# Attention's PSUM banks given out one by one, with the two sub-heads as separate steps in a new order

## The reference, cut to what matters

```python
attn1 = _attn(q1, k1, v)            # softmax(q1 k1^T / 4) v
attn2 = _attn(q2, k2, v)
attn = attn1 - lambda_full * attn2
rms = jax.lax.rsqrt(jnp.mean(attn * attn, axis=-1, keepdims=True) + EPS)
attn = attn * rms * subln_w * (1.0 - LAMBDA_INIT)
return attn.reshape(b, t, 512) @ wo.T
```

## Time and profile before

| what | value |
|---|---|
| median of three runs | 2588.03 us (2586.67 to 2591.05) |
| the profiled execution: own time, span | 2588.56 us, 2586.8 us |
| mean granted TensorE clock | 0.974 |
| busy share of the span: PE, DVE, ACT, POOL | 94%, 66%, 46%, 7% |
| heads of L0's attention (first exponential to last) | 184 to 1071 us |
| heads of L1's attention | 1847 to 2432 us |
| page, exponentials (line 565) | 896, 932 ns each on average |
| page, sums (line 494) | 2 x 3584 records, 560 ns each |

### The profile page before, as it was taken

The page is one execution under the profiler, slowest core; times in us unless marked ns, Lnnn a source line. Parts: engine busy times, 40 slices in busy tenths (PEclk is TensorE's granted clock), DMA queues, the critical chain, the costliest instruction groups (busy, mean ns, idle before and its releaser), DMA issues. The chain is left out here.

```text
span 2586.8 us, 41795 instructions
## 1 busy us (share of the span) xinstructions
PE 2424.4 (94%) x15600; PEld 1274.4 (49%) x15600; DVE 1705.7 (66%) x3976; ACT 1178.8 (46%) x1571; POOL 186.2 (7%) x341
## 2 busy tenths in 40 slices
PE   6899999999999999888999999968899999999886
PEld 5662333333333333367888888757533333333465
DVE  2247888888888888483444444442478888888586
ACT  2125656556656656652222122231255555555553
POOL 3000000000000000100000000000011111111103
PEclk9899999999999999899999999979899999999998
DMA  5654222122222200001000000005512122210001
GB/s 192 152 127 94 44 26 26 26 40 36 26 26 26 26 2 2 30 1 49 25 25 24 24 24 24 1 0 150 107 37 36 24 39 39 39 21 2 26 1 66
DMA packets 56669, 108.96 MB, mean 42 GB/s; under 512 B 11820, under 2 KB 22060, under 8 KB 56488
## 3 DMA queue, kind: packets, MB, share of 16 engines
q1 hardware_dynamic: 53960, 96.84, 19.0%
q0 software_dynamic: 2528, 9.70, 1.1%
HBM read 73.75 MB, written 31.46 MB: 41 GB/s over the span
## 5 line engine op out<-in xcount | busy, mean ns | idle before, releaser
L565 ACT ACTIVATE l_w_hi_prob<-l_p_work 128x1024 f32<-128x1024 f32 (+2 forms) x896 | 802.1, 932 | 535.4 <-PE l_p_work L472 535.3
L617 DVE TENSOR_REDUCE l_maxima<-l_p_ring 128x1 f32<-128x512 f32 x1280 | 824.3, 686 | 201.4 <-PE l_p_ring L447 179.5
L494 PE MATMUL l_p_work<-l_w_hi_prob,v_all 128*32 128x512 f32 (+3 forms) x3584 | 860.1, 560 | 8.7 <-ACT l_w_hi_sums L556 1.5
L494 PE MATMUL l_p_work<-l_w_hi_prob,l_ones 128*32 128x512 f32 (+3 forms) x3584 | 854.7, 560 | 0.0
L447 PE MATMUL l_p_ring<-xT_all 48*128 48x512 f32 (+3 forms) x1680 | 375.4, 443 | 11.9 <-DVE l_maxima L614 11.9
L447 PEld LDWEIGHTS l_p_ring<-xT_all 48*128 48x128 f32 x1680 | 157.6, 184 | 427.7 <-DVE l_maxima L617 244.0
L472 PE MATMUL l_p_work<-xT_all 50*128 50x512 f32 (+3 forms) x1680 | 325.3, 407 | 0.2 <-DMA xT_all<-l_shift_rows 0.2
L614 DVE CUSTOM_DVE_ANT_0 l_masked_scores<-l_p_ring,l_mask 128x128 bf16<-128x128 f32 (+3 forms) x512 | 230.7, 488 | 88.3 <-PE l_p_ring L447 79.0
L494 PEld LDWEIGHTS l_p_work<-l_w_hi_prob,v_all 128*32 128x32 f32 x3584 | 148.1, 108 | 282.6 <-issue 180.2
L472 PEld LDWEIGHTS l_p_work<-xT_all 50*128 50x128 f32 x1680 | 157.8, 185 | 186.7 <-ACT l_w_hi_prob L565 103.5
L1085 DVE SCALAR_TENSOR_TENSOR ffn_h<-ffn_p_u,ffn_group_scales,ffn_silu 128x512 f32<-128x512 f32 x64 | 48.1, 751 | 213.7 <-PE ffn_p_u L214 207.9
(11 more groups left out here) (149 smaller groups left out, 2870.9 us busy)
## 6 DMA issues: line engine op xcount, KB each, us to landing
xT_all<-q_parts SPq DMA_DIRECT2D x180, 128.0 KB
q_parts<-l_part SPq DMA_DIRECT2D x64, 256.0 KB
xT_all<-k_parts SPq DMA_DIRECT2D x90, 128.0 KB
k_parts<-l_part SPq DMA_DIRECT2D x40, 256.0 KB
xT_all<-k_parts SPq DMA_DIRECT2D x90, 64.0 KB
x<-in_x_T SPq DMA_DIRECT2D x4, 1024.0 KB, 11.2
x<-in_L_attn_x POOLq DMA_DIRECT2D x1, 4096.0 KB, 16.2
out<-x SPq DMA_DIRECT2D x16, 256.0 KB, 2.0
```

The lines of the kernel that those rows point to most:

```text
L494: summing = pe.matmul(p_out[r0:r0 + VD, off:CH], lhs, prob[step % PRING][:, sub, off:CH], start=first, stop=final)
L565: act.activation(prob[step % PRING][:, :, off:CH], p_score[:, step % 2, :, off:CH], ACT.Exp, scale=HD ** -0.5).then_inc(exped, 1)
L617: dve.tensor_reduce(to, scores, AX.X, ALU.max).then_inc(freed, 1)
```

## The change

- Every item that took two banks is now two items of one bank. `pair` becomes `maxima` of one sub-head (letters Q for sub-head 0, R for sub-head 1, P still for both); `score` takes a sub-head (letters U and V take the next one, S two). Each of these matmuls now waits and signals by itself.
- Banks: `p_ring` has four instead of three; scores have three single banks instead of two times two; `p_out` one. In the projections, q, k and value tiles share one ring of four work banks instead of three and two.
- The exponential is one instruction of up to 128 x 512 for each sub-head, twice as many as before. `prob` still has four buffers of both sub-heads, and a sum waits for both.
- `sums` has a buffer for each query half, so `copy_out` waits for the transposes of the same half one head earlier; the copies stand 4 and 3 half-steps (L0) or 3 and 2 (L1) behind.
- `keep` does one multiplication over both sub-heads (256 elements) instead of two (128 each).
- New order strings. Played out, one steady head of L0 has 16 sums in 10 runs of W (before: 16 runs), 64 row-half matmuls in 11 runs of R (before: 32 groups in 16 runs), and the two turns next to each other. One head of L1 has 12 sums in 8 runs of W (before: 9) and its row halves in 9 runs of R (before: 11).

```diff
-RING = 3
+RING = 4
+SCORE_BANKS = 3
+WORK_BANKS = 4
-QK_BANKS = 3
-V_BANKS = 2
...
+        done = {"score": [SUM_LAG] * 2, "maxima": [self.first_pairs] * 2, "sum": 0, "shift": 1}
...
+                if what in "SUV":
+                    for _ in range(2 if what == "S" else 1):
+                        take("score", S, 0 if done["score"][0] == done["score"][1] else 1)
+                elif what in "PQR":
+                    for sub in {"P": (0, 1), "Q": (0,), "R": (1,)}[what]:
+                        take("maxima", U, sub)
...
+L0 = Layer("l0", D, D, False, "VUQWWPRSUWRQVQVVWRQRUUQWUUURRQWQURSQWWXURUVRQWUVRQVQWWRVRQSWWQVSPTTRVSWWWVQR",
+           24, (4, 3))
+L1 = Layer("l1", D // 4, D // 4, True, "PVRWSQVTQRVUVRWWWUUQRVQWRURWXQRUQUVWRUQVWUVURQRQWTQVRVUWWWQUV",
+           20, (3, 2))
...
+            def take_bank(item):
+
+                if L.bank_at[item] >= RING:
+                    pe.wait_ge(freed, L.bank_at[item] - RING + 1)
+
+            def pair(n, u, subs=(0, 1)):
...
+                for sub in subs:
+                    take_bank(("maxima", n, u, max(subs)))
...
                 filling.then_inc(filled, 1)
...
-                if step >= 2:
-                    pe.wait_ge(exped, step - 1)
-                for sub in range(2):
-                    rows = slice(HALF * sub, HALF * sub + FROWS)
-                    scoring = pe.matmul(p_score[:, step % 2, sub, off:CH],
-                                        k[i][rows, L.k_head(n), kt * P:(kt + 1) * P],
-                                        q[i][rows, n % 2, qc * CH + off:(qc + 1) * CH], start=True, stop=True)
-                scoring.then_inc(scored, 1)
+                i, at = slot(n // 2), 2 * (n * S + s) + sub
+                if at < SCORE_BANKS:
+
+                    pe.wait_ge(v_kept, NT - WORK_BANKS + 1 + at)
+                else:
+                    pe.wait_ge(exped, at - SCORE_BANKS + 1)
+                if s == 0 and sub == 0:
+                    pe.wait_ge(shift_in, 64 * (n + 1))
+                rows = slice(HALF * sub, HALF * sub + FROWS)
+                pe.matmul(p_score[:, at % SCORE_BANKS, off:CH], k[i][rows, L.k_head(n), kt * P:(kt + 1) * P],
+                          q[i][rows, n % 2, qc * CH + off:(qc + 1) * CH], start=True, stop=True).then_inc(scored, 1)
...
-                if n + qc:
-                    before = ("turn", n, qc - 1) if qc else ("turn", n - 1, QC - 1)
-                    act.wait_ge(filled, L.filled_at[before])
-                act.activation(sums[:, :], p_out[:, :], ACT.Copy).then_inc(out_copied, 1)
+                if n:
+                    act.wait_ge(filled, L.filled_at["turn", n - 1, qc])
+                act.activation(sums[:, qc, :], p_out[:, :], ACT.Copy).then_inc(out_copied, 1)
...
-                act.activation(prob[step % PRING][:, :, off:CH], p_score[:, step % 2, :, off:CH], ACT.Exp,
+                act.activation(prob[step % PRING][:, sub, off:CH], p_score[:, at % SCORE_BANKS, off:CH], ACT.Exp,
                                scale=HD ** -0.5).then_inc(exped, 1)
...
-                dve.tensor_tensor(half[:, 0, :, :], cols[:, :, 0, 0:VD], recip[:, :, 0:1].to_broadcast([P, QPC, VD]),
-                                  ALU.mult)
-                dve.tensor_tensor(half[:, 1, :, :], cols[:, :, 1, 0:VD], recip[:, :, 1:2].to_broadcast([P, QPC, VD]),
+                dve.tensor_tensor(half[:, :, :, :], cols[:, :, :, 0:VD], recip[:, :, :, :].to_broadcast([P, QPC, 2, VD]),
                                   ALU.mult).then_inc(freed, 1)
```

More of the change, by code:

```diff
@@ L104, in __init__ @@
         self.filled_at, self.bank_at = {}, {}
-        bank = 0
+        bank = fills = 0
         for item in self.items:
-            if item[0] in ("pair", "shift", "turn"):
-                self.bank_at[item] = bank
-                self.filled_at[item] = len(self.bank_at)
-                bank += 2 if item[0] == "pair" else 1
+            if item[0] == "pair":
+                self.bank_at["maxima", *item[1:], 0], self.bank_at["maxima", *item[1:], 1] = bank, bank + 1
+                fills += 1
+                self.filled_at["maxima", *item[1:], 0] = self.filled_at["maxima", *item[1:], 1] = fills
+                bank += 2
+            elif item[0] in ("maxima", "shift", "turn"):
+                fills += 1
+                self.bank_at[item], self.filled_at[item] = bank, fills
+                bank += 1
     def projections(self):
@@ L139, in heads, with take @@
         S, U = len(self.steps), len(self.pairs)
-        out, scores, sums, pairs, shifts = [], 0, 0, self.first_pairs, 1
-        turns = []
-        while scores < SUM_LAG:
-            out.append(("score", *divmod(scores, S)))
-            scores += 1
+        done = {"score": [SUM_LAG] * 2, "maxima": [self.first_pairs] * 2, "sum": 0, "shift": 1}
+        out, turns = [("score", *divmod(i, S), sub) for i in range(SUM_LAG) for sub in range(2)], []
+        def take(name, size, sub):
+            at = done[name][sub]
+            done[name][sub] += 1
+            if at < HEADS * size:
+                out.append((name, *divmod(at, size), sub))
         for _ in range(HEADS):
             for what in self.pattern:
-                if what == "S" and scores < HEADS * S:
-                    out.append(("score", *divmod(scores, S)))
-                    scores += 1
-                elif what == "P" and pairs < HEADS * U:
-                    out.append(("pair", *divmod(pairs, U)))
-                    pairs += 1
-                elif what == "X" and shifts < HEADS:
-                    out.append(("shift", shifts))
-                    shifts += 1
+                if what in "SUV":
[4 more added lines that the diff above has]
+                        take("maxima", U, sub)
+                elif what == "X" and done["shift"] < HEADS:
+                    out.append(("shift", done["shift"]))
+                    done["shift"] += 1
                 elif what == "T" and turns:
@@ L538, in _ @@
                     pair(*at)
+                elif what == "maxima":
+                    pair(*at[:2], at[2:])
                 elif what == "score":
@@ L589, in _, with reduce @@
                 for qc, s in enumerate(L.qc_last):
[L590 to L594 removed]
+                    at = 2 * (n * S + s) + 1 + L.copied_after[qc]
+                    copies.setdefault(min(at, 2 * HEADS * S - 1), []).append((n, qc))
+            for at in range(2 * HEADS * S):
+                exp(*divmod(at // 2, S), at % 2)
+                for done in copies.get(at, []):
+                    copy_out(*done)
         @block.vector
         def _(dve):
[L598 removed]
+            def reduce(n, u, subs=(0, 1)):
                 qt, kc, keys, masking = L.pairs[u]
[L600 removed]
                 if u == 0 and n >= 2:
                     dve.wait_ge(shift_made, n - 1)
[L604 to L605 removed]
+                for sub in subs:
+                    dve.wait_ge(filled, L.filled_at["maxima", n, u, sub])
                     to = maxima[:, n % 2, sub * KT + qt, kc:kc + 1]
[L607 removed]
+                    scores = p_ring[:, L.bank_at["maxima", n, u, sub] % RING, 0:keys]
                     if masking:
@@ L612, in reduce @@
                         if before:
-                            dve.wait_ge(freed, L.bank_at["pair", before[0], before[1]] + sub + 1)
+                            dve.wait_ge(freed, L.bank_at["maxima", before[0], before[1], sub] + 1)
                         dve.tensor_tensor_reduce(masked_scores[sub][:, 0:keys], scores, mask[:, CH - keys:CH], 1.0, MASKED,
@@ L619, in make_shift @@
             def make_shift(n):
-                dve.wait_ge(freed, L.bank_at["pair", n, U - 1] + 2)
+                dve.wait_ge(freed, max(L.bank_at["maxima", n, U - 1, sub] for sub in range(2)) + 1)
                 if n:
@@ L656, in keep @@
                 dve.scalar_tensor_tensor(
-                    out=to, in0=half[:, 1, :, :], scalar=neg_lambda, in1=half[:, 0, :, :],
+                    out=to, in0=half[:, :, 1, :], scalar=neg_lambda, in1=half[:, :, 0, :],
                     op0=ALU.mult, op1=ALU.add).then_inc(out_kept, 1)
```

95 lines of the change are left out of this document (39 added, 56 removed).

## The result

The changed kernel takes 2480.72 us (median of 4 runs, 2479.18 to 2483.78); the kernel before took 2587.51 on the same chip. The ratio is 0.9587, with a 95% interval of 0.9573 to 0.9601.

What follows compares the result with a forecast made beforehand. PE's own instruction stream was taken to bound L0, with L1 not so pure. 30 heads x (1.65 us in L0 + 0.88 in L1) = 76 off 2588.5 gives 2513; own range 2487 to 2530, with rivals 2485 to 2552.

Steps and rivals of the forecast that it cites:

- Prices and L0: L0 head: run 0.195 us fixed, further group 0.235, joined sum saves 0.14 besides the run; 27.95 becomes 26.2.
- the 0.1 of waits that I allowed: L0: maxima fall behind by some tenths in five tight cycles; 0.1 us a head allowed.
- What is won before it is lost there: Second head's wait for shift rows brought by DMA, 3.46 us in L0: earlier gains are lost, so 30 heads count, not 32.
- The bank's is cut or stays, between 0 and 0.56; I keep 0.5: L1's wait for a ring bank, 0.56 us a head before: 0.5 kept because vector work is the next thing due.
- the first rival: Vector engine sets the pace: L0 heads wait 0.56 us for a bank, L1 keeps bank and copy waits; 2545 us; chance 0.22.
- the 1.25 slots that I counted at 0.29: L1's odd-length runs need 19.25 slots in place of 18 for row halves taken singly: +0.29 us a head.
- Projections and edges: Stretches outside the heads: same matmuls on four shared work banks instead of three and two; between -3 and +3 us, taken as nothing.
- Signals: Each matmul's own wait and signal costs time: 0.70 us a head in L0, 0.53 in L1; 2550 us; chance 0.08.
- The slower rival: Weights no longer loaded ahead: 0.105 us per later slot, 21 in L0, about 10 in L1; 2611 us; chance 0.05.
- Shift rows in L1: They come late: from shift to next head's first score 6.5 us instead of 7.07, costing 17 us; 2530 us; chance 0.05.
- Exponentials: Two of 601 ns replace one of 1024 ns, 2.9 us a head more in L0, 2.2 in L1, hidden under PE.
- with nothing kept: L1 head with no bank wait kept: 16.9 us, against the 17.4 forecast.

Runs made afterwards that it cites:

- experiment 6: Changed kernel with L0's order replaced by sixteen plain repeats of a maxima pair, a score pair and one sum: 2538.18 us, ratio 0.9804.
- experiment 5: Changed kernel with the second head's shift rows issued ahead of the loads of the fourth and fifth pair of heads, both layers: 2473.18 us, ratio 0.9559.
- Experiment 10: Changed kernel with two more 128 x 256 multiplications on the vector engine in each turn, into unread scratch: 2495.45 us, ratio 0.9633.
- Experiment 3: Changed kernel with three ring banks instead of four, the eighth bank unused: 2618.09 us, ratio 1.0108.
- experiment 2: Kernel before, with only the projections' q, k and value tiles sharing four work banks instead of three and two: 2584.78 us, ratio 0.9979.
- experiment 9: Changed kernel with L1's order as twelve plain blocks of a pair, a score pair and a sum, shift in block 8: 2670.57 us, ratio 1.0327.
- experiment 1: Changed kernel with the order strings of the kernel before, on the new banks: 2731.35 us, ratio 1.0546.
- experiment 8: Changed kernel with two score banks instead of three: 2936.87 us in one run.
- experiment 12: Changed kernel with L1's order as twelve plain blocks of a pair, a score pair and a sum, shift in block 5: 2557.64 us, ratio 0.9887.
- experiment 4: Kernel before with only L0's order changed, to eight runs of two pairs and two scores, each followed by two sums: 2771.65 us in one run.

## Why the prediction was too high

**Prices and L0: right.** The fixed cost of a run, the slot and the join of sums were read from the trace before and hold in the rows after, within 0.2 us a head. The head came out at 26.21 for 26.2 counted, and that closeness is partly luck: the sums are 0.17 cheaper than counted and the row halves 0.21 dearer (experiment 6's table). About 0.14 of the latter stand in three runs a head of 0.95 us where the others take 0.91, so the 0.1 of waits that I allowed may well be there. Over the stage the gain is 46.4 and not 49.5, though each steady head gives 1.74: 30 heads would be 52. Counted from each head's first exponential to the next head's, the first two intervals shrink by only 0.4 and 1.5 (30.50 to 30.06, 29.50 to 28.03), which is 1.6 of the 6 that are missing. The other 4 stand at the end: the last head's exponentials take 23.7 us from the first start to the last, before 19.8. Why, I have not traced. At the front the shift rows are waited for longer than before; PE waits 5.22 us, before 3.1 (the same wait is 3.46 for the loader in the earlier trace rows):

```profile
203.72 1.19 PE L478 MATMUL l_p_work<-x_early_q,x_early_k 50*128 50x512 f32 x3 [5.22 <-DMA x_early_q<-l_shift_rows]
```

"What is won before it is lost there" was thus right, and experiment 5 shows the cause, with the wait gone: two large loads stand ahead of the small rows on SP's queue.

**Step that failed: "The bank's is cut or stays, between 0 and 0.56; I keep 0.5".** It rested on the vector engine's 88% load, the same view that the first rival rested on. The wait is gone (0 in place of 0.5, 15 us over 30 heads). Experiment 10 shows that this load did not have to mean a wait: more vector work than in the kernel after leaves L0 alone at 90% and costs L1 half a microsecond at 93%. Experiment 3 shows what decides instead: without the fourth bank the row halves of an L1 head take 1.8 us more, with the vector engine less busy (81% of the stretch from 1950 to 2250 us) than after the change. A wait for a bank is a matter of how far PE may run ahead, and the load says little about it. No run gives the old order a fourth ring bank, so how much of the old wait the bank alone would take away is not separated from the order. The rest of L1's surplus, some 9 us, are the 1.25 slots that I counted at 0.29 and that cost about 0.1, and sums cheaper by 0.13 a head. In all, 30 times 1.67 is the 50 us measured, with one offset in it: L1's second interval gives 4.1 (20.72 to 16.65, as its waits at the front shrink), and the last head gives less than the others. With this the rival in which the vector engine sets the pace is out as well.

**Step that failed: "Projections and edges ... between -3 and +3 us, taken as nothing".** I looked only at the work banks, "four tiles in flight are still no fewer", and not at who else uses banks there: the early maxima matmuls draw on the same ring, and one of them held up PE for 2.93 us. That gave 9.3 us at the start and 4.2 before L1. Experiment 3 takes back all of it by the ring alone, experiment 2 gives 1 us of the start by the work banks alone. The 4.2 before L1 I have only by experiment 3's total, not by single waits. The steady gains of 1.74 and 1.67 a head make 102 us over 30 heads, which is the forecast's own lower end of 2487; it is these edges that put the time below it. What I left out altogether is that a wait of PE costs more than itself, since the granted clock behind it is lower. The Trainium skill ("TensorE: Matmul & The Clock Gate", "What's actually happening") says that the array is throttled unless activity releases it; the windows of 0.76 and 0.89 above agree, and so does the 0.50 behind the wait in experiment 5.

**Signals: the rival is out.** In the kernel after nearly every slot has two signals. The slot is 0.24 and most runs of three take 0.90 or 0.91 against 0.90; experiment 6 isolates it, with runs of two slots at 0.67 as before for 14 of 16 runs a head. That is about 0.01 a run, 0.1 us a head, where the rival had 0.70. The Trainium skill's 26.3 ns for each further signal ("TensorE: Matmul & The Clock Gate", "The cost: per-tile semaphore tail") doesn't show in this stream: the page gives it as a tail behind packed matmuls, and here another slot follows; that this slot covers it is my reading, not shown.

**The slower rival is out.** Neighbours in the same row half and matmuls with waits of their own stand at 0.24, not at 0.34, and all row halves of an L0 head are 0.21 us over the count where this rival wanted at least 2.2 (21 x 0.105). **Shift rows in L1** come in time; experiment 9 shows what it costs where they don't. **Exponentials** are hidden as predicted, with heads that show no wait for them, but the margin is the bank count together with the order, and not ACT's share: experiments 1, 8 and 12 all wait for exponentials, in experiment 12 with the banks of the kernel after and ACT busy for 59%, where the kernel after has 68% and no wait.

**The parts depend on each other.** The new banks without longer runs give nothing in L0 (28.25), longer runs without the fourth ring bank lose (28.68 in experiment 3, over 33 in experiment 4), both give 26.21. The same holds in L1: 18.43 without the bank, 19.03 without the order, 16.61 with both. So no sum of single effects leads to the result; the count of PE's stream does, if the banks let it run. My forecast without any wait, 16.9 in L1, was the better one, and it stood in the text as "with nothing kept". Not separated by any run: how much of L1's gain is single sub-heads as such and how much the spacing of the string.

## What to carry to other kernels

Where one engine is full, price its stream from start to start of its records, fixed cost of a switch and cost of a further group apart, and then ask of each wait whether it comes from load or from too few buffers; only the second goes away with a bank, and the busy share doesn't tell which it is. A bank taken from one user for another changes every stage that draws on either, those ahead of the main loop too. A short transfer that something waits for belongs ahead of the long ones on its queue.

## What the runs showed of the hardware that was not expected

- Waits of PE of 1.3 us on the mean (longest 1.8), 22 of them from 1900 to 2400 us, stand with a granted clock of 0.87 there and of 0.90 in the first 300 us of it (experiment 9), between the levels of 1.2 and 2.4 GHz; sums' first-pass records there reach 1.06 us, where they are 0.62 at full clock. With the shift earlier these waits are gone, others of up to 0.6 us stay, and the clock is 1.00 (experiment 12). One wait of 2.58 us is followed by ten microseconds at 0.50 (experiment 5).
- The shift rows, a small transfer issued behind two large loads, kept PE waiting for 5.2 us in L0; issued ahead of them, no wait is seen there.
- Two matmuls in the two row halves that signal each by itself cost no more than a pair with one signal (0.67 for a run of two slots in experiment 6 as before, 0.91 for a run of three against 0.90).
